# A Perceiver block on one core: the outputs of all units as one pipeline, tile loads across the boundary of the two parts, the first group's rows loaded in the first pass

## The chip, the cores and the metric

One core of one Trainium2 chip runs the whole program. The time is the device time of one execution in microseconds; a kernel is timed in several executions, and their median counts. A profiled execution is one more, with its own time.

## What is computed

128 sequences of 32 tokens with 512 channels pass through three residual layers. All arrays are float32; `ln` is a layer norm without weights.

```python
x = x + xattn(ln(x), ctx_768)   # 16 heads, softmax over 257 context rows of 384 channels
x = x + attn(ln(x))             # gated delta rule, one state of 32x32 per head, a scan over 32 tokens:
#   S = S * a_t;  delta = (v_t - k_t S) * beta_t;  S = S + k_t delta;  y_t = q_t S
#   context = rmsnorm(y) * norm_w * silu(gate);  out = context @ Wo.T + bo
x = x + ffn(ln(x))              # 8 experts of 512x512, the best 2 of each token, softmax of their two logits
```

## The kernel before

The 128 sequences are 32 units of four sequences, 128 token rows each (`NU` = 32); four units are a group (`NG` = 8 groups). The work lies in two passes, each a block in which the five engines (PE, DVE, ACT, POOL and SP, which issues most DMAs) run their own instruction lists and meet by semaphores.

`first_pass` goes over the units: the cross attention of unit u, and beside it the projections of unit u-1. It leaves rows in device memory: `x1` (the first residual sum), `gate`, `qk` and `qsq` for the products, and for the delta rule `kk` and `vb`. DVE solves the delta rule for a group at a time, five units later, as 32 time steps (`time_step`, lines 159 to 173), and SP stores the `deltas` by quarters of the steps. The last turn (unit 32 in `turn`, lines 450 to 487, `last=True`) has only the second half of the last unit and the last quarter of group 6's steps. Group 7's steps are left to the second pass.

`second_pass` (line 1016) has for each unit an **output** job: `y` from `qk` and `deltas` (PE, `make_y`, L1539), its square (ACT, L1328), the mean (DVE, `weighted`, L1400 to L1406), the power -1/2 (POOL, L1301), the scaled context (DVE, L1411), its transposes and the product with `wo` (PE, L1545 and L117), the residual sum with `x1` (DVE, L1419), a layer norm, the expert logits, the choice of two experts (DVE, `choose`), ranks within each expert (PE), the unit's slots (DVE, `place`, L1465), and two indirect DMAs that scatter the rows, scaled by their share, to `slot_rows` by expert (POOL, L1284). A PE `turn` of unit w does pieces of units w+1, w-1 and w-3 in three thirds, so that the engines overlap.

Then come the expert **tiles** of 128 rows: SP loads a tile from `slot_rows` (L1168), PE turns it (`xs_bank`, L1545) and multiplies it by its expert (`mix`, L117), ACT moves it, SP stores it back (L1172). Which expert and which rows a tile has comes from lists that DVE makes (`list_tiles`, L1473 to L1492) when all units of a part are placed; PE and SP read them as register values.

The units are in two parts, 24 and 8 (`UNITS`), with 55 and 23 tiles (`TILES`). Part 0's outputs run alone, turns 0 to 26; turns 24 to 26 only finish units 21 to 23. Then its 55 tiles run, with part 1's turns 24 to 34 among them, 33 thirds from tile 27 on (`inserted`). While the first tiles run, DVE does group 7's time steps; at tile 28 SP stores these deltas, waits for the store and loads group 7. Then SP waits for part 1's lists and scatters, loads the second residual sum of four units, and part 1's 23 tiles run. From the last store of part 0 on, POOL gathers the two expert rows of each unit (L1291, lines 1309 to 1318), DVE adds them to the second residual sum, loaded again (L1180), and SP stores the result (L1189).

```python
def inserted(t):                                            # line 1130
    n = 3 * (UNITS[1] + 3)
    return [(FIRST[1] + i // 3, i % 3) for i in range(n) if INSERT_AT + i * (TILES[0] - INSERT_AT) // n == t]
for part in range(2):                                       # SP, line 1214
    sp.wait_ge(lists_ready, part + 1)
    for i in range(2):
        sp.wait_ge(scattered[i], 16 * (FIRST[part] + UNITS[part]))
for part in range(2):                                       # DVE, line 1501
    first, end = FIRST[part], FIRST[part] + UNITS[part]
    if part == 1:
        for t in range(N):
            time_step(dve, own, tiles, t, t).then_inc(steps_done, 1)
    for w in range(first, end + 4):
```

## Time and profile before

| | us |
|---|---|
| median of 3 runs | 3528.31 (3527.48 to 3530.06) |
| the profiled execution | 3519.57 |
| its span, first to last instruction | 3517.8 |
| PE busy | 3116.7 (89%) |
| DVE busy | 2048.0 (58%) |
| ACT busy | 1131.3 (32%) |
| POOL busy | 987.8 (28%) |
| mean granted TensorE clock | 0.952 of full speed |

The span leaves out 1.8 us around the first and the last instruction of the profiled execution. Busy time of PE is that of its matrix products; weight loads overlap them. Times in the rows below are microseconds from the span's start; "idle before" is the time in which that engine did nothing just ahead of the row, with what ended it. SPq is the issuing of a DMA by SP, not its data. The first pass takes the first 2810 us, and the second pass the rest.

### The profile page before, as it was taken

The numbers are of one execution on the slowest core, as the hardware profiler recorded it, in microseconds if no ns is written. First come the engines' busy times: TensorE is split into PE (matmuls) and PEld (weight loads), VectorE is DVE, ScalarE is ACT, GpSimd is POOL, SyncE is SP. The second block draws the span as 40 slices with busy tenths as digits, with TensorE's granted clock in tenths as the row PEclk, the third lists the DMA queues.
The fourth block names the chain that finished last, engine by engine and source line by source line (L and its number), as shares of the span: only waits on it lengthen the run. The fifth ranks groups of instructions, "written<-read, shape, count | busy, mean of one in ns | idle before, by whom it ended". The sixth has DMA issues, their size and how long they took to land. (4 is left out here: it accounts for less than half of the span.)

```text
span 3517.8 us, 102137 instructions
## 1 busy us (share of the span) xinstructions
PE 3116.7 (89%) x42226; PEld 2288.9 (65%) x42226; DVE 2048.0 (58%) x4203; ACT 1131.3 (32%) x2656; POOL 987.8 (28%) x895
## 2 busy tenths in 40 slices
PE   6999999999999999999999998999899678799975
PEld 5777776767776777777777776777667445444542
DVE  2323366666666666666666666666666658793323
ACT  2333333333333333333333333333333223322321
POOL 2222222222222222222222222222222157502334
PEclk9999999999999999999999999999999878799998
DMA  4222222222222222222222222222221299635469
GB/s 157 83 87 73 89 78 75 75 92 78 75 75 92 78 75 75 92 78 78 72 96 80 75 75 92 78 75 75 92 78 66 70 233 258 211 126 151 138 231 333
DMA packets 297925, 379.11 MB, mean 108 GB/s; under 512 B 159568, under 2 KB 212304, under 8 KB 296016
## 3 DMA queue, kind: packets, MB, share of 16 engines
q1 hardware_dynamic: 287184, 338.19, 30.0%
q0 software_dynamic: 10240, 33.56, 2.8%
q8 instruction: 397, 6.50, 0.8%
q14 instruction: 104, 0.85, 0.1%
HBM read 258.17 MB, written 189.01 MB: 127 GB/s over the span
## 5 line engine op out<-in xcount | busy, mean ns | idle before, releaser
L117 PE MATMUL ring<-cond_high,wkv_high 128*128 128x342 f32 (+1 forms) x1152 | 406.0, 352 | 44.2 <-issue 22.1
L593 ACT ACTIVATE k_t<-ring,kvb 128x342 f32<-128x342 f32 (+1 forms) x384 | 209.5, 546 | 518.2 <-PE ring L117 518.2
L117 PE MATMUL ring<-cond_high,wkv_low 128*128 128x342 f32 (+1 forms) x1152 | 369.0, 320 | 0.0
L117 PE MATMUL ring<-cond_low,wkv_high 128*128 128x342 f32 (+1 forms) x1152 | 368.7, 320 | 0.0
L662 ACT ACTIVATE prob<-score,neg_max 128x257 f32<-128x257 f32 x512 | 236.4, 475 | 314.9 <-DVE neg_max L782 314.9
L117 PE MATMUL ring<-wkv_high,cond_high 128*128 128x512 f32 x768 | 320.5, 417 | 0.0
L170 DVE TENSOR_TENSOR prod<-prod 128x256 f32<-128x256 f32 (+5 forms) x352 | 303.7, 863 | 12.1
L166 DVE TENSOR_TENSOR prod<-coef,deltas 128x64 f32<-128x64 f32 (+30 forms) x248 | 303.0, 1222 | 5.0
L117 PE MATMUL ring<-wkv_high,cond_low 128*128 128x512 f32 x768 | 303.4, 395 | 0.7 <-issue 0.7
L117 PE MATMUL ring<-wkv_low,cond_high 128*128 128x512 f32 x768 | 303.7, 395 | 0.0
L117 PE MATMUL mix<-experts,xs_t 128*128 x624 | 285.9, 602 | 0.0
L117 PEld LDWEIGHTS ring<-cond_high,wkv_high 128*128 128x128 f32 x1152 | 217.8, 189 | 95.9 <-issue 55.0
L895 PE MATMUL turned<-ident,prob 128*128 128x128 f32 x1024 | 152.1, 297 | 108.0 <-DVE prob L789 108.0
L117 PE MATMUL ring<-x1n_t,wattn 128*128 128x128 f32 x2048 | 239.0, 278 | 0.0
L117 PEld LDWEIGHTS ring<-x1n_t,wattn 128*128 128x128 f32 x2048 | 233.8, 194 | 0.0
L117 PE MATMUL ring<-wattn,x1n_t 128*128 128x512 f32 x512 | 230.2, 602 | 0.0
L117 PEld LDWEIGHTS ring<-cond_low,wkv_high 128*128 128x128 f32 x1152 | 218.1, 189 | 15.1 <-issue 15.1
L519 POOL TENSOR_TENSOR tick<-minus_half 128x1 f32<-128x1 f32 x124 | 25.0, 202 | 711.0 <-PE ring L117 711.0
L794 DVE COPY prob_t<-turned 128x512 f32<-128x512 f32 x128 | 88.6, 692 | 228.1 <-PE turned L895 228.1
L112 POOL TENSOR_TENSOR cond_low<-cond,cond_high 128x771 fp32r<-128x771 f32 x128 | 216.5, 1692 | 10.3
L895 PEld LDWEIGHTS turned<-ident,prob 128*128 128x128 f32 x1024 | 131.0, 153 | 134.9 <-DVE prob L789 121.8
L117 PEld LDWEIGHTS ring<-cond_high,wkv_low 128*128 128x128 f32 x1152 | 217.6, 189 | 0.0
(199 smaller groups left out, 5862.4 us busy)
## 6 DMA issues: line engine op xcount, KB each, us to landing
cond<-cond_t_dram SPq DMA_DIRECT2D x128, 385.5 KB, 4.0
xs<-slot_rows SPq DMA_DIRECT2D x78, 256.0 KB, 2.9
slot_rows<-ys SPq DMA_DIRECT2D x78, 256.0 KB, 2.1
x_rows<-x SPq DMA_DIRECT2D x64, 256.0 KB, 3.1
vb_rows<-vgb SPq DMA_DIRECT2D x64, 256.0 KB, 3.2
x_in<-x_dram SPq DMA_DIRECT2D x32, 256.0 KB, 4.7
v_last_s<-v_last_rows SPq DMA_DIRECT2D x512, 0.5 KB
kk_rows<-kk_rows_s SPq DMA_DIRECT2D x32, 256.0 KB, 2.7
```

Source lines behind the costliest of these rows:

```text
L112: return eng.tensor_tensor(low, whole, high.bitcast(F32), ALU.subtract)
L117: last = pe.matmul(out, lhs_t, rhs, start=(i == 0), stop=(i == len(terms) - 1))
L166: own.then(dve.tensor_tensor(tiles["prod"][:, 0:t], coef, tiles["deltas"][:, 0:t], ALU.mult))
L170: own.then(dve.tensor_tensor(tiles["prod"][:, 0:half], tiles["prod"][:, 0:half], tiles["prod"][:, left:whole], ALU.add))
L519: own = Own(pool, pool_steps, lambda: pool.tensor_tensor(tick[:], minus_half[:], minus_half[:], ALU.add))
L593: act.activation(k_t[:, group, at:at + n], ring_bank[bank][:, 0:n], ACT.Identity, bias=kvb[:, group:group + 1]).then_inc(ring.free[bank], 1)
L662: act.activation(prob[:, g, :], score[:, g, 0:M], ACT.Exp, bias=neg_max[:, g:g + 1], accum_out=sums[:, g:g + 1]).then_inc(exp_done, 1)
L794: dve.tensor_copy(prob_t[:, 1, :], turned[1][:]).then_inc(prob_t1_ready, 1)
L895: last = pe.transpose(turned[j][:, g * P:g * P + P], prob[:, g, j * P:j * P + P], ident[:])
```

## The change

It has four parts. One: `qk`, `delta` and `x1` of the second pass move into a tile `shared_rows` that holds the Q weights and the keys in the first pass; SP loads group 0's rows and four units' `x1` into it in the first pass's last turn, after three waits, and no longer at the second pass's start. Two: the turns of the second pass run from 0 to 34 in one line with no end at unit 24; turns 0 to 26 (`BEFORE` = 27) run ahead of the tiles, with everything of units 24 to 27 that falls into them, and turns 27 to 34, 24 thirds, are inserted from tile 32 to tile 49. DVE's group 7 steps come between turns 26 and 27. Three: the tiles run from 0 to 77 in one line; SP's wait for part 1's lists and scatters stands at tile 52, three ahead of the first tile that needs it, the store and load of group 7 at tile 29, the loads of the second residual sum after tile 55's store. Four: POOL sets only the constant -1/2 at first and makes the others after the first unit's bias; PE's waits for weights and constants move to the thirds that use them.

```diff
-INSERT_AT = 27
+BEFORE = NU - GU - 1
+INSERT_AT, INSERT_END = 32, 50
...
+        shared = both.enter_context(nc.sbuf_tensor("shared_rows", [P, DC * D + HG * MU], F32))
+        early = {"qk": shared[:, 0:BU * D].rearrange("p (b n) -> p b n", b=BU),
+                 "delta": shared[:, BU * D:2 * BU * D].rearrange("p (b n) -> p b n", b=BU),
+                 "x1": shared[:, 2 * BU * D:3 * BU * D].rearrange("p (b n) -> p b n", b=4),
...
-        wq = sb("wq", [P, DC, D])
+        wq = shared[:, 0:DC * D].rearrange("p (c n) -> p c n", c=DC)
...
-        k_t = sb("k_t", [P, HG, MU])
+        k_t = shared[:, DC * D:].rearrange("p (g n) -> p g n", g=HG)
...
+                if last:
+                    sp.wait_ge(x1_stored, 16 * NU)
+                    sp.wait_ge(qk_stored, 16 * (NU - 1))
+                    sp.wait_ge(deltas_stored, 16 * ((NG - 1) * GU - 1))
+                    load_group(sp, early, [early["qk"]], [early["delta"]], rows, 0)
+                    for w in range(4):
+                        load_x1(sp, early, rows["x1"], w)
                 if group is None:
                     store_results(u, (u - 1) // GU, (u - 1) % GU)
...
-        qk = sb("qk", [P, 2, BU, D])
-        delta = sb("delta", [P, 2, BU, D])
-        x1 = sb("x1_unit", [P, 4, D])
+        qk = [early["qk"], sb("qk", [P, BU, D])]
+        delta = [early["delta"], sb("delta", [P, BU, D])]
+        x1 = early["x1"]
...
-            n = 3 * (UNITS[1] + 3)
-            return [(FIRST[1] + i // 3, i % 3) for i in range(n) if INSERT_AT + i * (TILES[0] - INSERT_AT) // n == t]
+            n, places = 3 * (NU + 3 - BEFORE), INSERT_END - INSERT_AT
+            return [(BEFORE + i // 3, i % 3) for i in range(n) if INSERT_AT + i * places // n == t]
...
-            load_group(0)
             load_unit(0)
             sp.dma_start(bo_s[:], bo.rearrange("(a n) -> a n", a=1).to_broadcast([P, D])).then_inc(bo_loaded, 16)
-            load_x1(0)
...
-            for w in range(1, 4):
-                load_x1(w)
-            load_group(1)
-            for w in range(UNITS[0] + 2):
-                follow(w, FIRST[0], UNITS[0])
+            load_group(sp, early, qk, delta, rows, 1)
+            for w in range(BEFORE):
+                follow(w)
...
+            tiles_listed(0)
+            at = {t: row_of(t) for t in range(3)}
+            for t in at:
+                load_tile(t, at[t])
+            for t in range(sum(TILES)):
+                if t + 3 == START[1]:
+                    tiles_listed(1)
+                if t + 3 < sum(TILES):
+                    at[t + 3] = row_of(t + 3)
+                    load_tile(t + 3, at[t + 3])
+                if t == INSERT_AT - 3:
+                    sp.wait_ge(steps_done, N)
+                    store_deltas(sp, tiles, rows["deltas"], NG - 1, 0, N).then_inc(deltas_stored, 16)
+                    sp.wait_ge(deltas_stored, 16)
+                    load_group(sp, early, qk, delta, rows, NG - 1)
+                for w, third in inserted(t):
+                    if third == 2 and w < NU + 2:
+                        follow(w)
+                store_tile(t, at.pop(t))
+                if t == START[1]:
                     for i in range(2):
                         sp.wait_ge(x2_stored[i], 16 * NU // 2)
                     for w in range(4):
                         load_x2(w)
...
+            pool.memset(minus_half[:], -0.5).then_inc(half_ready, 1)
+            pool.wait_ge(half_ready, 1)
             pool.wait_ge(bo_loaded, 16)
...
+            for w in range(NU + 4):
...
+                if w == 0:
+                    make_constants()
+                if w + 1 == BEFORE:
+                    scatter(BEFORE - 4)
...
+            for w in range(NU + 4):
+                if w == BEFORE:
+                    place(w - 4)
+                    list_tiles(0)
                     dve.wait_ge(coef_loaded, 16)
                     dve.wait_ge(steps_loaded, 16)
                     for t in range(N):
                         time_step(dve, own, tiles, t, t).then_inc(steps_done, 1)
...
-            pe.wait_ge(outputs_loaded, 32)
-            pe.wait_ge(constants, 1)
-            for w in range(FIRST[0], UNITS[0] + 3):
+            for w in range(BEFORE):
                 for third in range(3):
-                    turn(w, third, FIRST[0], UNITS[0])
+                    if (w, third) == (1, 1):
+                        pe.wait_ge(outputs_loaded, 32)
+                    if (w, third) == (3, 2):
+                        pe.wait_ge(constants, 1)
+                    turn(w, third)
```

How the instructions move shows best in three places. The first is SP at the end of the first pass and the start of the second, where an unconditional branch leads from block to block. Before, the last turn's `x1` store and zero fill are followed by the last results, and group 0 comes after the branches:

```order
L427 DMA x_rows<-x 128x512
L453 DMA slot_rows<-zero_rows 9x4x16384
L435 DMA qsq_rows<-qsq 128x16
L436 DMA kk_rows<-kk_rows_s 128x8x64
L438 DMA qk_rows<-decay 128x512
L441 DMA vb_rows<-vgb 128x8x64 x2
L444 DMA gate_rows<-vgb 128x512
L145 DMA delta_rows<-deltas 128x384
L198 UNCONDITIONAL_BRANCH
L1135 UNCONDITIONAL_BRANCH
L1142 DMA qk<-qk_rows 32x4x512
L1144 DMA delta<-delta_rows 32x8x64 x4
```

Now the group's loads (one quarter of four is shown) and the `x1` loads stand between the zero fill and the results:

```order
L449 DMA x_rows<-x 128x512
L475 DMA slot_rows<-zero_rows 9x4x16384
L212 DMA shared_rows<-qk_rows 32x4x512
L214 DMA shared_rows<-delta_rows 32x8x64 x4
...
L204 DMA shared_rows<-x_rows 128x512 x4
L457 DMA qsq_rows<-qsq 128x16
L458 DMA kk_rows<-kk_rows_s 128x8x64
L460 DMA qk_rows<-decay 128x512
```

The 24 loads moved ahead of six stores of the first pass and of the branch.

The second place is PE at the last turns ahead of the tiles. Before, turns 25 and 26 have only transposes of `x2n`, logits and ranks, and the tiles' first transposes follow:

```order
L1545 MATMUL turn_bank<-ident,x2n 128x128 x4
L117 MATMUL small_bank<-gate,x2n_t 128x8 x4
L117 MATMUL small_bank<-member,earlier 128x8
L117 MATMUL small_bank<-taken,ones 128x8
L1545 MATMUL turn_bank<-ident,x2n 128x128 x4
L117 MATMUL small_bank<-gate,x2n_t 128x8 x4
L117 MATMUL small_bank<-member,earlier 128x8
L117 MATMUL small_bank<-taken,ones 128x8
L1580 MATMUL small_bank<-taken,ones 128x8
L1597 TENSOR_LOAD expert_at
L1597 ISA x2
L1545 MATMUL xs_bank<-ident,xs 128x128 x4
```

Now turn 26 is as full as the ones before it, with `y` of unit 27, the context of unit 25 and its product with `wo`:

```order
L1566 MATMUL turn_bank<-ident,x2n 128x128 x4
L1560 MATMUL y<-shared_rows 32x32 x64
L1566 MATMUL turn_bank<-ident,context 128x128 x4
L118 MATMUL small_bank<-gate,x2n_t 128x8 x4
L118 MATMUL wo_bank<-wo,context_t 128x512 x4
L118 MATMUL small_bank<-member,earlier 128x8
L118 MATMUL small_bank<-taken,ones 128x8
L1601 MATMUL small_bank<-taken,ones 128x8
L1621 TENSOR_LOAD expert_at
L1621 ISA x2
L1566 MATMUL xs_bank<-ident,xs 128x128 x4
```

Four `y` and two `wo` products came in here, ahead of the first tile.

The third place is PE at the last inserted third, that with unit 31's ranks and the totals (L1580 before, L1601 now). Before, part 0's last product stands right ahead of it and the first tile of part 1 right behind, with two tiles' transposes in a row, as at a start:

```order
L117 MATMUL mix<-experts,xs_t 128x512
L117 MATMUL small_bank<-member,earlier 128x8
L117 MATMUL small_bank<-taken,ones 128x8
L1580 MATMUL small_bank<-taken,ones 128x8
L1597 TENSOR_LOAD expert_at
L1597 ISA x2
L1545 MATMUL xs_bank<-ident,xs 128x128 x4
L1597 TENSOR_LOAD expert_at
L1597 ISA x2
L1545 MATMUL xs_bank<-ident,xs 128x128 x4
L117 ISA
L117 MATMUL mix<-experts,xs_t 128x512
```

Now a tile's transposes and products follow as after any third, and the boundary between the parts comes five tiles later:

```order
L118 MATMUL mix<-experts,xs_t 128x512
L118 MATMUL small_bank<-member,earlier 128x8
L118 MATMUL small_bank<-taken,ones 128x8
L1601 MATMUL small_bank<-taken,ones 128x8
L1621 TENSOR_LOAD expert_at
L1621 ISA x2
L1566 MATMUL xs_bank<-ident,xs 128x128 x4
L118 ISA
L118 MATMUL mix<-experts,xs_t 128x512
L118 ISA
L118 MATMUL mix<-experts,xs_t 128x512
```

The ranks moved ahead of tiles 50 to 54, and the start with two transposes in a row is gone.

## Rows read from the trace of the kernel before

**Rows 1.** Windows: us, busy us (and instructions) of each engine, granted clock, DMA share, GB/s.
```profile
2842.00:3043.00 201.00, 180.17 (x3272) 117.06 (x3272) 153.74 (x492) 68.51 (x144) 138.38 (x101) 0.86 0.90 248
...
3186.00:3365.00 179.00, 168.40 (x1580) 92.97 (x1579) 53.09 (x189) 57.60 (x111) 51.65 (x38) 0.98 0.45 144
...
3480.00:3518.00 38.00, 0.30 (x1) 0.00 (x0) 15.22 (x22) 0.60 (x1) 19.02 (x19) 0.55 0.86 295
...
3400.00:3490.00 90.00, 74.07 (x220) 34.21 (x218) 26.67 (x39) 20.79 (x37) 38.85 (x41) 0.97 1.00 353
```

**Rows 2.** Timeline of PE, second pass's start: start us, us, what, [idle before <-releaser].
```profile
2823.76 1.93 PE L1539 MATMUL y<-delta,qk 32*32 32x32 f32 x128 [27.53 <-DMA delta<-delta_rows]
2830.61 3.08 PE L1539 MATMUL y<-delta,qk 32*32 32x32 f32 x218 [4.92 <-DMA gate<-gate_t_dram]
...
2841.72 4.72 PE L117 MATMUL wo_bank<-wo,context_t 128*128 128x512 f32 x6 [0.69 <-ACT context_t L1334]
```

**Rows 3.** Timeline of SP's DMA issues, end of the first pass and start of the second.
```profile
2763.55 0.82 SPq L453 DMA_DIRECT2D slot_rows<-zero_rows  x1
2793.76 0.36 SPq L435 DMA_DIRECT2D qsq_rows<-qsq  x1
...
2810.28 0.35 SPq L1142 DMA_DIRECT2D qk<-qk_rows  x1
...
2820.61 0.45 SPq L1149 DMA_DIRECT2D silu_unit<-gate_rows  x1
...
2826.33 0.50 SPq L1142 DMA_DIRECT2D qk<-qk_rows  x1
...
2841.52 0.45 SPq L1149 DMA_DIRECT2D silu_unit<-gate_rows  x1
```

**Rows 4.** Timeline of DVE: two products with the gate (L1406), two units' slots (L1465).
```profile
2891.64 0.69 DVE L1406 TENSOR_TENSOR context<-y,silu_unit 128x512 f32<-128x512 f32 x1
...
2952.19 0.68 DVE L1406 TENSOR_TENSOR context<-y,silu_unit 128x512 f32<-128x512 f32 x1
...
3042.93 0.17 DVE L1465 CAST slots<-slot 128x2 uint32<-128x2 f32 x1
...
3066.99 0.17 DVE L1465 CAST slots<-slot 128x2 uint32<-128x2 f32 x1
```

**Rows 5.** Timeline of PE around the hold of SP.
```profile
3201.58 1.29 PE L1539 MATMUL y<-delta,qk 32*32 32x32 f32 x128
3202.80 0.65 PE L1545 MATMUL turn_bank<-ident,context 128*128 128x128 f32 x4
...
3207.43 3.60 PE L117 MATMUL wo_bank<-wo,context_t 128*128 128x512 f32 x8
3216.47 1.11 PE L1545 MATMUL xs_bank<-ident,xs 128*128 128x128 f32 x4 [5.45 <-DMA xs<-slot_rows]
```

**Rows 6.** Timelines of DVE after its time steps, and of SP around the hold.
```profile
3188.15 0.69 DVE L1400 TENSOR_REDUCE mean_sq<-y_sq 128x16 f32<-128x512 f32 x1 [6.88 <-ACT y_sq L1328]
...
3193.76 0.33 SPq L1168 DMA_DIRECT2D xs<-slot_rows  x1
...
3213.30 0.34 SPq L1168 DMA_DIRECT2D xs<-slot_rows  x1
```

**Rows 7.** Timeline of PE at the boundary between the parts.
```profile
3380.23 1.11 PE L1545 MATMUL xs_bank<-ident,xs 128*128 128x128 f32 x4 [14.65 <-DMA xs<-slot_rows]
...
3383.00 4.52 PE L117 MATMUL mix<-experts,xs_t 128*128 x8
...
3387.80 3.60 PE L117 MATMUL mix<-experts,xs_t 128*128 x8
...
3391.67 1.88 PE L117 MATMUL mix<-experts,xs_t 128*128 x4
```

**Rows 8.** Timeline of SP at the boundary.
```profile
3370.86 1.76 SPq L1180 DMA_DIRECT2D deltas<-x_rows  x4
```

**Rows 9.** The page's part 5, ACT's moves of the keys: busy us, mean ns | idle before, releaser.
```profile
L593 ACT ACTIVATE k_t<-ring,kvb 128x342 f32<-128x342 f32 (+1 forms) x384 | 209.5, 546 | 518.2 <-PE ring L117 518.2
```

More of the change, by code:

```diff
@@ L1013, in _, with second_pass @@
             turn(NU, last=True)
[L1016 removed]
+def second_pass(nc, ident, early, rows, wo_t, bo, gate_t, expert_t, out):
     with ExitStack() as ctx:
@@ L1149, in load_unit, with follow @@
                     sp.dma_start(dst[:, w % 2], rows[name][unit_rows(w), :]).then_inc(unit_loaded[w % 2], 16)
-            def load_x1(w):
-                sp.dma_start(x1[:, w % 4], rows["x1"][unit_rows(w), :]).then_inc(x1_loaded[w % 4], 16)
-            def follow(w, first, end):
-                if w < end and w + 2 < NU:
+            def follow(w):
+                if w + 2 < NU:
                     sp.wait_ge(y_read, w + 1)
                     load_unit(w + 2)
-                if first <= w - 2:
+                if w >= 2:
                     sp.wait_ge(x2_ready, w - 1)
@@ L1498, in combine @@
                 dve.tensor_tensor(found[:, w % 4, 0], found[:, w % 4, 0], x2_again[:, w % 4], ALU.add).then_inc(out_ready, 1)
-            dve.wait_ge(constants, 1)
-            for part in range(2):
-                first, end = FIRST[part], FIRST[part] + UNITS[part]
-                if part == 1:
+            dve.wait_ge(half_ready, 1)
+            for w in range(NU + 4):
+                if w == BEFORE:
+                    place(w - 4)
+                    list_tiles(0)
                     dve.wait_ge(coef_loaded, 16)
@@ L1508, in _ @@
                         dve.wait_ge(steps_done, t + 1)
-                for w in range(first, end + 4):
-                    if first <= w - 1 < end:
-                        normalised(w - 1)
-                    if first <= w - 2 < end:
-                        residual(w - 2)
-                    if first <= w - 4:
-                        place(w - 4, part)
-                    if w < end:
-                        weighted(w)
-                    if first <= w - 2 < end:
-                        statistics(w - 2)
-                    if first <= w - 3 < end:
-                        choose(w - 3, first)
-                    if first <= w - 2 < end:
-                        scaled(w - 2)
-                list_tiles(part)
+                if 0 <= w - 1 < NU:
+                    normalised(w - 1)
+                if 0 <= w - 2 < NU:
+                    residual(w - 2)
+                if w >= 4 and w != BEFORE:
+                    place(w - 4)
+                if w < NU:
+                    weighted(w)
+                if 0 <= w - 2 < NU:
+                    statistics(w - 2)
+                if w == 3:
+                    dve.wait_ge(constants, 1)
+                if 0 <= w - 3 < NU:
+                    choose(w - 3)
+                if 0 <= w - 2 < NU:
+                    scaled(w - 2)
+            list_tiles(1)
             for w in range(NU):
@@ L1567, in turn @@
                             .then_inc(logits_ready, 1)
-                    if first <= w - 1 < end:
+                    if 0 <= w - 1 < NU:
                         pe.wait_ge(context_moved, w)
@@ L1573, in turn @@
                             .then_inc(wo_ready, 1)
-                if third == 2 and first <= w - 3:
+                if third == 2 and w >= 3:
                     r = w - 3
@@ L1624 @@
+            pe.wait_ge(experts_loaded, 16 * E)
+            expert = expert_of(0)
+            turn_tile(0)
+            for t in range(sum(TILES)):
+                if t + 1 < sum(TILES):
+                    following = expert_of(t + 1)
+                    turn_tile(t + 1)
+                mix_tile(t, expert)
+                expert = following
+                for w, third in inserted(t):
+                    turn(w, third)
 INPUTS = ["x", "cond_t", "cond_last_t", "q_w", "q_b", "kv_w", "kv_b", "proj_w", "proj_b", "attn_w_t", "wa_t",
```

215 lines of the change are left out of this document (92 added, 123 removed).

## The prediction

> **What bounds the kernel now.** I read four views. First the page: PE is busy 89% of the 3517.8 us, and its row of 40 slices is at 8 or 9 tenths through the first pass; the five slices below 8 tenths that are not the first are the first pass's end and parts of the second pass. The change moves work only there, so I cut the second pass into stretches [rows 1]: outputs (2842 to 3043), tiles with inserted outputs (3186 to 3365), the last 23 tiles with DMA engines in full use (within 3400 to 3490) and the tail. In the outputs PE is busy 180 of 201 us at a mean clock of 0.86, with the DMA engines at 0.90: nearly everything is full. In the inserted stretch PE is busy 168 of 179 us: PE sets the time. From 3400 to 3490 the DMA engines are at 1.00 and move 353 GB/s: there bytes set the time as much as PE. Then timelines of PE, SP and DVE around each joint, which follow with the terms.
>
> **Term 1, the start of the second pass.** PE's first output product waits 27.5 us for the first group's rows, and 4.9 us more for the gate weights; the first Wo product starts at 2841.72 [rows 2]. SP shows why [rows 3]: at 2810.28 it starts 20 loads for group 0 (four quarters of one load and four small ones), which take it until 2820.61, then 11 others, then group 1's 20 until 2841.52, and only then the loads of units 2 and 3. The change issues group 0 and four x1 loads in SP's idle time in the first pass: SP has nothing between 2763.55+0.82 and 2793.76. The 24 issues cost 10.3 us (group 0's price) plus 4 at 0.52 us (11 issues from 2820.61 to 2826.33): 12.4 us, up to 17 at the price that group 1's issues had when the queue was full. They end near 2784, ten us before SP's next issue, so I price them at nothing; what covers them is DVE's last time steps, and without that cover 12 to 17 us would return. Their waits are for stores issued no later than 2763.
> What is left ahead of group 1 is 7 issues, 3.6 us, so group 1 starts at 2813.9 and ends 10.3 to 15.2 us later, at 2824 to 2829 instead of 2841.5: 13 to 18 us earlier, and units 2 and 3 with it. On PE's own side, 13.5 us of the first wait lie after 2810.28, and with the 4.9 us 18 would go. The queue is the later of the two: I take **-16 us**, range -9 to -18 (-9 if the DMA engines, at 0.90 through the outputs, let through only what the 3 MB moved out are worth at 353 GB/s, 8.9 us). Moving the constants on POOL behind the first bias delays unit 1 by a few us at a point where PE still waits on unit 0: nothing.
>
> **Term 2, turns 24 to 26.** Today these drain: unit 19's slots are written at 3042.93 and unit 23's at 3066.99, four turns in 24.1 us [rows 4]. With four more output products and two more Wo products they run like full turns. Seven full turns lie between 2891.64 and 2952.19: 8.65 us each. Four take 34.6 us: **+10 us** (0 if the added work fell wholly into the drain's gaps; +14 if PE's whole 13.7 us for it, worked out in term 3, came on top).
>
> **Term 3, less to insert.** The same work leaves the tile stretch: four output products and two units' transposes and Wo products. The rows are 1.29, 0.65 and 3.60 us [rows 5]; 4x1.29 + 2x(0.65+3.60) = 13.7 us, and the wait for ACT before each Wo product, 0.69 us [rows 2], makes it 15. I take **-15 us** (-13 to -17, as other waits go with it or stay). PE is full there, so all of it counts.
>
> **Term 4, the hold of SP.** SP stores the last group's deltas, waits, and issues that group's 20 loads between the load of tile 31 (3193.76) and of tile 32 (3213.30): 19.5 us in which no tile is loaded or stored [rows 6]. PE lives on the three tiles already loaded and on inserted work, and idles 5.45 us [rows 5]. After the change the hold comes one tile later, and the first inserted turn only at tile 32, behind the hold. Nothing fills it but three tiles: the inserted work of that stretch (1.29 + 0.65 + 3.60, and one more 1.29) is no longer cover. **+6.5 us** (0 to +10). The time steps that the hold waits for are done before it in both: DVE idles 6.9 us before 3188.15 [rows 6].
>
> **Term 5, the boundary between the parts.** Between the last tile of part 0 and the first of part 1 PE idles 14.65 us, then two transposes, and the product starts at 3383.00 [rows 7]: 17.4 us from 3365.6. SP starts part 1's loads only once the lists and the last scatter are there (3370.86) [rows 8], which is 5.3 us after PE's last rank product. In the changed kernel that product sits behind tile 49, SP reaches the wait at tile 52, two tiles and a store later, 2x3.87+1 = 8.7 us (the tile pitch is 3391.67-3387.80 [rows 7]). 5.3 is under 8.7: the wait costs nothing, tile 55 is loaded as any other, and **-17 us** follow (-8 if lists and scatter come 9 us later).
>
> **Term 6, the tail.** From the first product of part 1 to the end are 134.8 us now. The first gathers and the first four tile and x2 loads ran in the hole, beside no tile; they now run beside tiles. What comes after part 0's last store is 64 gathers, 32 loads and 32 stores of a unit and 46 tile moves, 174x262,144 bytes = 45.6 MB; at 353 GB/s that is 129 us, and the last 38 us run at 0.86. Near 138 us instead of 134.8: **+3 us** (0 to +10). A rule speaks for more. In the Trainium skill, "DMA: Bandwidth & Descriptors", section "Queues, rings and completion order", each DMA engine takes turns between the queues that have work. By it the eight gathers that start at once would leave SP's queue half the rate, some 176 GB/s by rows 1: tiles 55 to 57 with their x2 loads are 2.6 MB, 15 us instead of 11.6, and the term +6. No row of this trace has that overlap, so the sum goes by the total of bytes.
>
> **Sum.** -16 + 10 - 15 + 6.5 - 17 + 3 = -28.5 us. The profiled execution took 3519.57 us and would take 3491; the median of the runs shown is 3528.31, 8.7 above it, and I carry the difference over: 3499.8, rounded **3500 us**. What a measurement of this kernel can tell from no change is about 0.2%, 7 us.
>
> **Rivals.**
> *The boundary turns into a hold of another kind.* SP's new wait stands ahead of the store of tile 52, so every us that lists and scatters come later than 8.7 us stops stores, then PE; or the gathers that now start at once take the tile loads' bandwidth. For it: the DMA engines at 1.00 from 3400 on. Against: the 5.3 us. If it gives back 12 of the 17 us: 3512 us.
> *The outputs are limited by bytes.* For it: 0.90 DMA share over 201 us. Against: PE also at 90%, and the even 8.65 us turns. Then terms 1 and 2 become -9 and +14: -17.5, 3511 us.
> *The change does less than it says.* One drain, between outputs and the first tile, stays as it is; if the start stays bound by the first unit's chain and the boundary drain only moves to tile 52, terms 1 and 5 shrink to -6 and -5: about -6.5, 3522 us, no change to a measurement.
> *Slower.* The first pass's Q weights and keys move into one tile ahead of all others, so every later tile gets a new address. If that made each of the 31 full turns of the first pass 1.2 us longer, 37 us would come on top: 3537 us. The point from which it decides is 28.5/31 = 0.9 us a turn. For it nothing; against it, the 384 key moves that write there (546 ns in the mean) have 518.2 us of ACT's idle time before them, all of it waiting on PE [rows 9], so a longer move would be hidden.
>
> **How the numbers follow.** Forecast 0.62, boundary 0.15, bytes 0.11, does less 0.06, slower 0.06. The bounds of the terms rarely fall together; half of each way gives about 14 us to the fast side, 3486, and the rivals at 3511 and 3512 need the slow end at 3515. Faster than 0.2%: the first three, 0.88; same 0.06; slower 0.06.
>
> **What would show it.** The first Wo product near 2823 us of the span; unit 23's slots near 3060; first tile product near 3072; one PE idle near 12 us at tile 32; no PE idle over 2 us between tiles 54 and 55; the first product of tile 55 near 3350; the end near 3489. Wrong if the first pass ends later than 2812, if PE's idle at tile 52 to 55 is over 8 us, or if the stretch from tile 55 to the end is over 145 us.

## The result

The changed kernel takes 3500.98 us (median of 4, 3496.33 to 3502.64) and the kernel before 3529.18 (median of 4, 3527.48 to 3534.02): the ratio given with the result is 0.9904, 95% interval 0.9889 to 0.9918, and the two medians alone divide to 0.9920. Forecast were 3500 us and 3486 to 3515. In a second set, on one chip, it was 3496.08 (6 runs) against 3530.99 (11 runs): ratio 0.9907, interval 0.9888 to 0.9926. So the change gains 28 to 35 us, 0.8 to 1.0%.

### The profile after

The profiled execution of the changed kernel took 3502.01 us (span 3500.2), only 17.6 less than that of before. That gap between profiles and medians is the first thing to explain; the stage table below does it. First the lines that answer to those shown of before.

Windows of the changed kernel: outputs, tiles with inserted turns, the last 23 tiles, the tail (columns as in [rows 1]):

```profile
2832.00:3035.00 203.00, 182.31 (x3335) 118.55 (x3337) 152.50 (x492) 68.41 (x144) 137.69 (x101) 0.85 0.85 246
3188.00:3360.00 172.00, 157.68 (x1053) 86.81 (x1052) 44.67 (x180) 54.49 (x107) 38.34 (x33) 0.96 0.46 150
3390.00:3460.00 70.00, 64.85 (x195) 30.05 (x194) 21.80 (x32) 19.00 (x33) 30.50 (x33) 1.00 1.00 358
3462.00:3500.00 38.00, 0.59 (x2) 0.00 (x0) 15.22 (x22) 0.60 (x1) 18.97 (x19) 0.54 0.88 301
```

The stages are the same and as full as before [rows 1]: TensorE (PE) at 90% of the outputs, DMA engines at 1.00 beside the last tiles. What changed is at the joints.

TensorE at the start of the second pass (answers to [rows 2]):

```profile
2813.30 1.45 PE L1560 MATMUL y<-shared_rows 32*32 32x32 f32 x90 [12.73 <-PEq L220]
2816.66 1.88 PE L1560 MATMUL y<-shared_rows 32*32 32x32 f32 x128 [1.90 <-issue]
2823.69 1.88 PE L1560 MATMUL y<-shared_rows 32*32 32x32 f32 x128 [5.16 <-issue]
2829.08 0.75 PE L1560 MATMUL y<-shared_rows 32*32 32x32 f32 x38 [3.51 <-issue]
...
2831.66 6.38 PE L118 MATMUL wo_bank<-wo,context_t 128*128 128x512 f32 x8 [0.78 <-ACT context_t L1356]
```

The first output product starts the moment the second pass does and waits for no rows. But three pauses without any wait ("issue"), 10.6 us in sum, stand before the first Wo product. Before, there was one such pause in the same place, in a row that [rows 2] leave out:

```profile
2839.24 0.75 PE L1539 MATMUL y<-delta,qk 32*32 32x32 f32 x38 [5.55 <-issue]
```

So 5 of the 10.6 us are new.

SP over the same time, the moved loads in the first pass included (answers to [rows 3]):

```profile
2766.47 0.82 SPq L475 DMA_DIRECT2D slot_rows<-zero_rows  x1
2768.13 0.34 SPq L212 DMA_DIRECT2D shared_rows<-qk_rows  x1
...
2770.45 5.88 SPq L212 DMA_DIRECT2D shared_rows<-qk_rows  x1
...
2785.50 1.89 SPq L204 DMA_DIRECT2D shared_rows<-x_rows  x4
2796.70 0.34 SPq L457 DMA_DIRECT2D qsq_rows<-qsq  x1
...
2813.27 0.34 SPq L1171 DMA_DIRECT2D silu_unit<-gate_rows  x1
...
2832.02 0.45 SPq L1171 DMA_DIRECT2D silu_unit<-gate_rows  x1
```

The 24 moved issues take 2768.13 to 2787.4, 19 us where up to 17 were priced (one alone 5.88), and end 9 us before SP's next issue at 2796.70: the cover held. The store of zeros just ahead of them already stands 2.9 us later than before, so the second pass starts 3.0 us later (2813.27) for a reason ahead of the change.

TensorE and SP at the hold (answer to [rows 5] and [rows 6]):

```profile
3204.00 3.60 PE L118 MATMUL mix<-experts,xs_t 128*128 x8
3217.52 1.11 PE L1566 MATMUL xs_bank<-ident,xs 128*128 128x128 f32 x4 [9.92 <-DMA xs<-slot_rows]
3218.43 5.79 PE L118 MATMUL mix<-experts,xs_t 128*128 x8
```

```profile
3197.75 0.33 SPq L1187 DMA_DIRECT2D xs<-slot_rows  x1
3198.13 0.43 SPq L146 DMA_DIRECT2D delta_rows<-deltas  x1
3203.19 0.34 SPq L212 DMA_DIRECT2D qk<-qk_rows  x1
...
3214.40 0.37 SPq L1187 DMA_DIRECT2D xs<-slot_rows  x1
```

SP loads no tile for 16.65 us (19.5 before), with nothing inserted to cover it, and TensorE idles 9.92 us in place of 5.45. The product behind this idle takes 5.79 us where others take 3.60; the granted clock from 3217.5 to 3222 is 0.50, the lower of its two levels (1.2 and 2.4 GHz).

TensorE at the boundary of the parts and behind it (answers to [rows 7]; the products are those of tiles 54, 55 and 58, the transposes those of tiles 56 and 59):

```profile
3356.36 3.60 PE L118 MATMUL mix<-experts,xs_t 128*128 x8
3359.80 0.60 PE L1566 MATMUL xs_bank<-ident,xs 128*128 128x128 f32 x4
3360.24 3.60 PE L118 MATMUL mix<-experts,xs_t 128*128 x8
...
3376.49 1.11 PE L1566 MATMUL xs_bank<-ident,xs 128*128 128x128 f32 x4 [4.92 <-DMA xs<-slot_rows]
3377.40 4.81 PE L118 MATMUL mix<-experts,xs_t 128*128 x8
```

Tile 54 (3356.36) and tile 55 (3360.24) follow each other at the tiles' pitch. Three tiles later TensorE idles 4.92 us on a late tile load, and the product behind it takes 4.81 us; no profile of before has an idle over 1.6 us behind its first tiles there.

### The stages, over several profiles

S is SP's first DMA issue of the second pass. Each stage is the difference of two times of the timelines: S, the slots of units 19 and 23 (DVE), ACT's moves of the products of tiles 26 and 54, the end. In us:

| profile | S | S to first Wo | S to unit 19 | 19 to 23 | 23 to tile 26 | tile 26 to 54 | 54 to end | S to end |
|---|---|---|---|---|---|---|---|---|
| before | 2810.3 | 31.4 | 232.6 | 24.1 | 119.2 | 178.8 | 152.8 | 707.5 |
| before, second | 2807.2 | 31.7 | 240.4 | 24.8 | 119.2 | 186.1 | 154.5 | 725.0 |
| before, third | 2818.0 | 31.4 | 238.7 | 24.3 | 118.8 | 186.5 | 155.5 | 723.9 |
| changed | 2813.3 | 18.4 | 221.7 | 34.3 | 119.0 | 171.7 | 140.2 | 687.0 |
| changed, second | 2809.5 | 20.0 | 218.2 | 32.2 | 119.6 | 171.0 | 142.0 | 683.0 |

The first profile of before is 17 us quicker behind S than the two others. Read against all three, the second pass gained 34 us, not 20.

### The profile page after: what moved, and what is told of

Same layout as the page of the kernel before. It is cut to its first block and busy times, and to the rows that moved or that the text cites. A ratio compares the mean times of both kernels' runs of the same rounds, so it can differ in the third digit from the quotient of the medians.

```text
span 3500.2 us, 102140 instructions
## 1 busy us (share of the span) xinstructions
PE 3121.0 (89%) x42226; PEld 2290.5 (65%) x42226; DVE 2048.1 (59%) x4203; ACT 1130.3 (32%) x2656; POOL 987.8 (28%) x895
## 5 line engine op out<-in xcount | busy, mean ns | idle before, releaser
L622 ACT ACTIVATE shared_rows<-ring,kvb 128x342 f32<-128x342 f32 (+1 forms) x384 | 209.3, 545 | 516.9 <-PE ring L118 516.7
L171 DVE TENSOR_TENSOR prod<-prod 128x256 f32<-128x256 f32 (+5 forms) x352 | 301.5, 857 | 12.1
L548 POOL TENSOR_TENSOR tick<-minus_half 128x1 f32<-128x1 f32 x124 | 24.8, 200 | 709.3 <-PE ring L118 709.3
```

The costliest lines, as they stand in the source:

```text
L171: own.then(dve.tensor_tensor(tiles["prod"][:, 0:half], tiles["prod"][:, 0:half], tiles["prod"][:, left:whole], ALU.add))
L548: own = Own(pool, pool_steps, lambda: pool.tensor_tensor(tick[:], minus_half[:], minus_half[:], ALU.add))
L622: act.activation(k_t[:, group, at:at + n], ring_bank[bank][:, 0:n], ACT.Identity, bias=kvb[:, group:group + 1]).then_inc(ring.free[bank], 1)
```

## The experiments

**before_again and before_third.** The kernel before, unchanged, profiled twice more.

> The kernel before, profiled a second time. The two profiles shown are 17.6 us apart (3519.6 and 3502.0), the medians 28.2 us. If the profiled execution of before shown was a short one by chance, this one lies nearer its median, at 3525 to 3532, and the extra 5 to 12 us lie in stages that the change doesn't touch. If profiled executions of before are always short, it is 3520 again. The store of the last x1 rows in the first pass, issued at 2763.1 in before and 2766.1 in the changed kernel, tells whether the first pass differs between the kernels: at 2763 again the shared addresses lengthen the first pass by 3 us, at 2766 or more it is chance.

> The kernel before, profiled a third time, for the spread of its stages. From the two profiles at hand: second pass's first issue to unit 19's slots 232.6 and 240.4 us, moves of tile 26 to tile 54 (the stretch with the inserted turns) 178.8 and 186.1, move of tile 54 to the end 152.8 and 154.5. If the stretch with the inserted turns is what scatters, by windows in which TensorE's granted clock falls below 1.00, it comes out between 176 and 188 here, longer the more such windows it has, and the tail stays at 152 to 155; if the scatter is spread over all stages alike, the tail moves too.

Spans 3532.2 and 3541.8, executions of 3534.0 and 3543.6 us: longer than the 3525 to 3532 that I expected, and longer in stages that the change does touch. The first profile was a short one, and the places where it was short are the outputs (232.6 against 240.4 and 238.7) and the stretch with the inserted turns (178.8 against 186.1 and 186.5). The tail moves by 3 us only. The windows of 100 us behind tile 31, first of the profile of before, then of the second and the third:

```profile
3222.00:3272.00 50.00, 48.74 (x544) 27.14 (x543) 13.06 (x49) 16.36 (x32) 11.37 (x8) 1.00 0.45 144
3272.00:3322.00 50.00, 48.35 (x424) 26.96 (x423) 18.40 (x70) 17.52 (x35) 20.21 (x15) 1.00 0.40 133
```

```profile
3228.00:3278.00 50.00, 47.10 (x529) 25.82 (x528) 10.79 (x42) 15.31 (x30) 11.36 (x8) 0.97 0.41 138
3278.00:3328.00 50.00, 47.15 (x413) 26.06 (x412) 17.41 (x63) 15.76 (x31) 20.20 (x15) 0.97 0.37 122
```

```profile
3236.00:3286.00 50.00, 47.05 (x529) 25.82 (x528) 10.51 (x41) 14.97 (x30) 11.36 (x8) 0.97 0.43 137
3286.00:3336.00 50.00, 46.65 (x413) 26.19 (x412) 17.70 (x65) 16.20 (x31) 20.10 (x15) 0.97 0.37 122
```

The quick profile has the clock at 1.00 throughout and TensorE at 97%; the others have a mean of 0.97 and TensorE at 94%. Behind the hold an idle came ahead of the lower clock; whether an idle or the clock came first in these windows, no run tells. As for the first pass: the store of the last x1 rows is issued at 2760.0 and 2770.8 in these two profiles, and S lies at 2807 to 2818 in the three profiles of before and at 2807 to 2821 in the eleven of the changed kernel and its variants, so the 3 us of the first pair are within the scatter, and the shared addresses cost nothing that shows.

**after_again, start_undone, boundary_undone**, on one chip.

> The changed kernel again, as the base of the next two runs: 0.990 of before. By chance in the first pass its store of the last x1 rows moves by a few us; if the shared addresses are the cause, it stays at 2766. No PE idle over 2 us at tiles 52 to 55, about 5 us of idle at tile 58, and about 10 at tile 32.

Measured: 3496.08 us, S at 2809.5, no idle at tiles 52 to 55, 4.75 us at tile 58, 9.54 at tile 32: all as in the first profile of this kernel, and the first pass's 3 us gone.

start_undone takes the moved loads out of the last turn and puts them back at the second pass's start:

```
-                if last:
...
-                    load_group(sp, early, [early["qk"]], [early["delta"]], rows, 0)
-                    for w in range(4):
-                        load_x1(sp, early, rows["x1"], w)
...
+            load_group(sp, early, qk, delta, rows, 0)
             load_unit(0)
...
+            load_x1(sp, early, rows["x1"], 0)
...
+            for w in range(1, 4):
+                load_x1(sp, early, rows["x1"], w)
             load_group(sp, early, qk, delta, rows, 1)
```

> The changed kernel with group 0's rows and the first four x1 rows loaded at the second pass's start again. By the prediction's term the time rises by 16 us over the changed kernel. By the lower end of that term (the transfers of the start are limited by bytes) it rises by 9. By the profile of the changed kernel, where the first product of the second pass comes 13 us earlier behind its start, it rises by 13 and the first product stands 28 us behind the pass's first issue, as before. By the rival of the shared addresses (slower first pass), which stay in this kernel, nothing of the first pass changes.

Measured: 3508.17 us (6 runs, 3500.54 to 3509.92), 12.1 over the changed kernel. Its stage from S to unit 19 is 233.0, 13 over the mean of the two profiles of the changed kernel (220.0); the others stay. So the early rows are worth 12 to 13 us: between the two bounds of the term. TensorE's rows in it:

```profile
2819.93 3.08 PE L1557 MATMUL y<-shared_rows 32*32 32x32 f32 x218 [27.04 <-DMA shared_rows<-delta_rows]
2827.27 1.88 PE L1557 MATMUL y<-shared_rows 32*32 32x32 f32 x128 [4.26 <-issue]
2833.48 0.75 PE L1557 MATMUL y<-shared_rows 32*32 32x32 f32 x38 [4.34 <-issue]
```

The first 218 products come in one piece here, and the first pause is missing; in the changed kernel the first piece is 90 products, then 1.9 us of pause. What TensorE took in while it waited for rows, it now has to wait for by itself.

boundary_undone drains SP, TensorE and ScalarE between tiles 54 and 55 (SP's part of the edit):

```
-                if t + 3 < sum(TILES):
+                if t + 3 < START[1] or START[1] <= t < sum(TILES) - 3:
                     at[t + 3] = row_of(t + 3)
                     load_tile(t + 3, at[t + 3])
...
                 store_tile(t, at.pop(t))
-                if t == START[1]:
+                if t + 1 == START[1]:
+                    tiles_listed(1)
...
+                    for i in range(START[1], START[1] + 3):
+                        at[i] = row_of(i)
+                        load_tile(i, at[i])
```

> The changed kernel with a drain between tiles 54 and 55 as before: x2 loads and the tile loads of the second part follow the store of tile 54, and TensorE and ScalarE take up tile 55 behind tile 54's product. By the prediction's terms for the boundary (17) and the tail (gives back 3) the time rises by 14; by the rival that the boundary's gain goes to gathers and bytes behind it, it rises by 5 at most, since the tail from the first product of tile 55 to the end shrinks from 140 us to 125 or so. PE idles 10 to 15 us ahead of tile 55 in both; the tail's length tells.

Measured: 3504.72 us (6 runs), 8.6 over the changed kernel; the stage from tile 54 to the end is 149.8, 8.7 over the mean of the two (141.1). TensorE ahead of tile 55:

```profile
3349.35 7.03 PE L118 MATMUL mix<-experts,xs_t 128*128 x16
3364.55 1.11 PE L1570 MATMUL xs_bank<-ident,xs 128*128 128x128 f32 x4 [8.17 <-DMA xs<-slot_rows]
```

8.17 us of idle where before had 14.65 [rows 7]: since the inserted turns end at tile 49, lists and scatters are long there, and this drain is shorter than the old one. So of the 13 us that the last stage lost (154.3, the mean of the three of before, to 141.1), 8.7 are the missing drain, and some 4 are left for the earlier end of the turns, which no run tried by itself. Neither theory had that split: one gave 14, the other 5 at most.

**group1_late, hold_spread, x2_early, stores_later**, in a later set. These four take up the pauses, the hold and the idle at tile 58.

```
             load_unit(1)
-            load_group(sp, early, qk, delta, rows, 1)
             for w in range(BEFORE):
                 follow(w)
+                if w == 1:
+                    load_group(sp, early, qk, delta, rows, 1)
```

> The changed kernel with group 1's twenty loads issued behind unit 3's (they are first needed by turn 3) and not ahead of unit 2's. Theory A, transfers hold up the start: TensorE's gaps between the pieces of the first three y (1.9 to 2.7, 4.9 to 5.2 and 3.0 to 4.6 us in three profiles of kernels with the early rows, with no wait to explain them) shrink with 1.3 MB less under way, the first Wo product comes 3 to 6 us sooner behind the second pass's first issue (18 to 20 us in those profiles), and the whole gains as much. Theory B, TensorE's own intake of instructions sets the gaps: they stay at 10 us in sum, the first Wo product stays at 18 to 20 us, and the time is the changed kernel's within 0.1%, since unit 2's rows, though 12 us sooner, wait behind the first residual on VectorE. Theory C: group 1 comes too late for turn 3, and y of unit 4 waits: 3 to 8 us slower.

Measured: 3495.06 us (6 runs): the changed kernel's time. TensorE's rows:

```profile
2812.24 1.46 PE L1561 MATMUL y<-shared_rows 32*32 32x32 f32 x90 [12.30 <-PEq L220]
2815.59 1.88 PE L1561 MATMUL y<-shared_rows 32*32 32x32 f32 x128 [1.90 <-issue]
2822.90 1.88 PE L1561 MATMUL y<-shared_rows 32*32 32x32 f32 x128 [5.43 <-issue]
2826.37 0.75 PE L1561 MATMUL y<-shared_rows 32*32 32x32 f32 x38 [1.59 <-issue]
```

Unit 2's rows are issued at 2818.61, 6.4 us behind S and not 18.8, and the first Wo product still comes 16.7 us behind S. So SP's queue is not what holds the start: Theory B in the main. Of Theory A one trace is left: the last pause, beside which no transfer of group 1 runs now, is 1.59 us, against 2.4 to 4.6 in the nine other profiles with early rows, while the middle one, beside Wo's megabyte, stays at 5.43. Theory C fell.

```
-                if t == INSERT_AT - 3:
+                if t == INSERT_AT - 6:
                     sp.wait_ge(steps_done, N)
                     store_deltas(sp, tiles, rows["deltas"], NG - 1, 0, N).then_inc(deltas_stored, 16)
+                if INSERT_AT - 4 <= t < INSERT_AT:
                     sp.wait_ge(deltas_stored, 16)
-                    load_group(sp, early, qk, delta, rows, NG - 1)
+                    load_group(sp, early, qk, delta, rows, NG - 1, [t - INSERT_AT + 4])
```

(Here `load_group` takes the quarters that it is to load as one more argument.)

> The changed kernel with the last deltas stored at tile 26 and group 7 loaded five rows at a time at tiles 28 to 31, and not both at tile 29. If SP's hold of 17 us costs the idle of 9.5 to 10 us on TensorE at tile 32, as my term for the hold has it, that idle goes to under 2 us, and the time falls by 8 to 11 us with the product at a low clock behind it. If the y of group 7 would have waited there anyway (deltas stored late), the idle moves to the first y of turn 27 and less than 3 us is gained.

Measured: 3490.11 us (5 runs), 5.0 under group1_late beside it and 6.0 under the changed kernel's 3496.08; in the trace the idle is gone and the stage from tile 26 to 54 is 160.6, 10.8 under the 171.4 of the changed kernel (mean of two):

```profile
3207.16 3.60 PE L118 MATMUL mix<-experts,xs_t 128*128 x8
3210.60 0.60 PE L1567 MATMUL turn_bank<-ident,x2n 128*128 128x128 f32 x4
3211.61 1.29 PE L1561 MATMUL y<-delta,qk 32*32 32x32 f32 x128 [0.41 <-DMA delta<-delta_rows]
```

The first y of group 7 waits 0.41 us: the hold, not the deltas, had been the cost. The trace shows all that was expected; the medians show 5 to 6 us of the 8 to 11, and scatter over 7 to 13 us.

x2_early changes one number (`if t == START[1] - 4:` for the four x2 loads), stores_later another (`- 5` in place of `- 2` in `combined`).

> The changed kernel with the first four x2 rows loaded at tile 51 and not at 55. If the idle of 4.8 us at tile 58 comes from transfers that share the engines (x2's 1 MB, eight gathers of 256 KB and the tiles' rows at once), 1 MB less leaves 2 us of idle, and the tail from the move of tile 54 to the end (140 to 142 us in two profiles) shrinks by 2 to 3 us, which are 1 MB at 360 GB/s. If SP's wait for the first combined unit causes it (the store of unit 0's output stands in SP's queue ahead of tile 60's load), the idle stays, and the tail too.

> The changed kernel with each store of a combined unit three tiles later in SP's order. If SP's wait for the first combined unit causes the idle at tile 58, the idle goes, but the gathers behind the stores start 12 us later, so the tail from the move of tile 54 to the end is longer or as long: what limits it is bytes (0.96 to 1.02 of the transfer engines from 3390 on). If TensorE's tiles set the end of the tail, the idle goes and the tail shrinks by 5 us. If transfers cause the idle, it stays at 3 to 5 us.

Measured: x2_early 3493.56 us (6 runs), the idle at tile 58 gone, tail 135.2 us: 5.9 less, twice what 1 MB is worth at 360 GB/s. The idle of 4.92 us and the 1.2 us that the product behind it took too long (4.81 for 3.60) make that up. In the medians it is 2.5 us under the changed kernel and 1.5 under group1_late, which 6 runs each don't tell from nothing. TensorE at the place:

```profile
3367.84 3.60 PE L118 MATMUL mix<-experts,xs_t 128*128 x8
3371.31 0.63 PE L1566 MATMUL xs_bank<-ident,xs 128*128 128x128 f32 x4
3371.77 3.60 PE L118 MATMUL mix<-experts,xs_t 128*128 x8
```

stores_later 3503.32 us (6 runs): the idle stays (4.69), and the tail is 152.2, 11 longer. So the four x2 loads cause the idle, not SP's wait for the first combined unit. Whether it is by their bytes alone no run tells: in the changed kernel their issues also take SP 1.87 us (from 3364.94) just ahead of tile 59's load (3367.55). And whoever stores later gathers later.

**hold_and_x2, x2_kept and eight_places.** The two edits that helped, together; then with x2 of 16 units kept in buffers that are read out; then with eight places for gathered units and x2 of 8 units kept. Of the last two edits the main lines:

```
+        keep = [early["qk"], early["delta"], qk[1], delta[1]]
...
+            def keep_x2(w):
+                sp.wait_ge(y_ready, 28 if w < 12 else 32)
+                sp.wait_ge(x2_stored[w % 2], 16 * (w // 2 + 1))
+                sp.dma_start(x2_at(w), rows["x2"][unit_rows(w), :]).then_inc(x2_kept[(w - 4) // 8], 16)
```

```
+        keep = [qk[1], delta[1]]
+        places = [found[:, i] for i in range(4)] + [early[n][:, 2 * i:2 * i + 2] for n in ("qk", "delta") for i in range(2)]
```

> The changed kernel with both edits that helped: group 7's rows spread over tiles 28 to 31 (stretch of the inserted turns 171 to 160.6 us), and the first x2 rows at tile 51 (tail from the move of tile 54 to the end 141 to 135 us). If the two costs are apart from each other, both gains add: 10.5 + 6 = 16 us below the changed kernel, 3481. If the tail is limited by the bytes it must move alone, whenever TensorE gets there, the tail is 135 again; if it was limited by when part 1's tiles come, it grows.

> The former, with x2 of units 4 to 19 loaded into the buffers of groups 6 and 7 when these are read out (tiles 4 to 11 and 42 to 49), where the transfer engines are at half share or less, so that 4 MB fewer move in the tail. If bytes limit the tail, it loses 4 MB at 360 GB/s, 11 us: from 135 to 124, and the whole comes to 3470. If the round trips of the four gather buffers limit it (gather, sum, store, each waiting for the one before), it stays over 131. If TensorE's 23 tiles at 3.87 us and the last units behind them limit it, it ends at 125 to 130.

> The kernel with both edits (group 7's rows spread, the first x2 rows at tile 51; 3487.0 us, tail from the move of tile 54 to the end 135.6 us), with eight places for gathered units in place of four (four of them in the buffers of group 6, read out before the tiles) and x2 of units 4 to 11 kept in those of group 7. The tail took 135.4 us with 4 MB fewer to move, so bytes alone don't set it. If the round trips of the four places do (gather, two sums, store, each behind the one before), the tail falls to 118 to 128, and the whole to 3470 to 3480. If the tiles' own loads and stores and the orders of SP set it, it stays at 133 to 137. If sixteen gathers at once hold up the tiles' loads, TensorE idles by over 5 us behind tile 58, and the tail is 135 to 145.

Measured: hold_and_x2 3487.02 us (4 runs; ratio to before 0.9863, interval 0.9841 to 0.9885), stages 164.0 and 135.6: the gains add in the trace but for 3 us, while the median is 9 us under the changed kernel, and 16 were expected. x2_kept 3484.44 (4 runs) and eight_places 3483.96 (4 runs) were expected at 3470, and at 3470 to 3480: they gain 3 us more, which 4 runs each don't tell from nothing. Their tails are 135.4 and 134.9. The first rules out bytes as the only limit and left the round trips (over 131). The second rules out the round trips as the only limit; it fits the tiles' own loads and stores and SP's orders (133 to 137), and its TensorE still idles, 4.33 us behind tile 59 and 2.57 two tiles on. Windows from the move of tile 55 or so to the last tile, and from there to the end, of hold_and_x2, x2_kept and eight_places:

```profile
3360.00:3454.00 94.00, 86.75 (x261) 40.45 (x259) 29.07 (x42) 24.73 (x43) 43.28 (x46) 1.00 0.98 345
3454.00:3491.00 37.00, 0.58 (x2) 0.00 (x0) 15.23 (x22) 0.60 (x1) 19.55 (x18) 0.56 0.89 303
```

```profile
3354.00:3447.00 93.00, 87.28 (x260) 41.47 (x258) 29.07 (x42) 24.10 (x43) 43.72 (x46) 0.98 0.91 305
3447.00:3485.00 38.00, 0.37 (x1) 0.00 (x0) 15.22 (x22) 0.60 (x1) 18.33 (x19) 0.54 0.87 293
```

```profile
3347.00:3446.00 99.00, 89.56 (x261) 42.05 (x259) 31.94 (x47) 24.48 (x43) 48.58 (x48) 0.97 0.93 320
3446.00:3478.00 32.00, 0.25 (x1) 0.00 (x0) 11.73 (x17) 0.60 (x1) 15.53 (x16) 0.58 0.88 310
```

With fewer bytes the share falls (0.98 to 0.91) but not the time: bytes are not what is left of the tail. With eight places the part behind the last tile is 5 us shorter and the tiles ahead of it 4 to 6 longer, while sixteen gathers start beside them. What is left of the 135 us is then the 23 tiles at 3.87 us (89), transfers in their way (8 to 14), and a chain of 32 to 38 behind the last tile, where the last eight units are gathered and those and the ones ahead of them summed and stored. That chain took 37 to 38 us in the kernel before too, so nothing that the change gained in the last stage came from there. It was not tried apart, and stays open.

## Why the prediction was right, and which steps were not

The total came out within a microsecond of the first median and 4 over the second. By its own steps, with the forecast, the first pair of profiles, and the means of the profiles in the table (3 of before, 2 of the changed kernel):

| terms | forecast | first pair | means |
|---|---|---|---|
| 1, to unit 19 | -16 | -10.9 | -17.3 |
| 2, unit 19 to 23 | +10 | +10.2 | +8.8 |
| 3 and 4, tile 26 to 54 | -8.5 | -7.1 | -12.4 |
| 5 and 6, tile 54 to end | -14 | -12.6 | -13.2 |

**The frame.** The sum was made against a profile 8.7 us under the median, and the 8.7 were carried over. That worked by luck in part. For the profile the sum gave 3491 us, and 3502.01 was measured: it promised 28.5 us, and the first pair shows 17.6. The median came out because the changed kernel's profile lies 1.0 us over its median and not 8.7 under. The three profiles of before differ by 24 us. A sum that is made against one execution has its scatter in every term that is a stretch and not a gap. So the signs in the profile came late: the first Wo product at 2831.66 for 2823, unit 23's slots at 3069 for 3060, the first product of tile 55 at 3360.24 for 3350, the end at 3500.2 for 3489, with 3.0 us of each from the first pass.

**Term 1** is right in its sign and mis-sized: with the loads put back the kernel is 12.1 us slower, not 16. The step that failed is "The queue is the later of the two". SP's queue did come free 9.5 us sooner in the profile (2841.52 to 2832.02), and 12.5 sooner behind S, close to the 13 to 18 forecast; but making it free 12 us sooner still (group1_late) changed the median by 1.0 us, within the scatter. TensorE's side is the later: the forecast had it lose 18 us, 13.5 for rows and 4.9 for the gate weights. The rows' part came true. The wait for the gate weights went too, but the pauses grew by as much, from one of 5.55 us to three of 10.6 us in sum, and the forecast had no room for the new ones: from the first y to the first Wo product it is 18.4 us now and was 18.0. So it lost 13.0 in the first pair (31.4 to 18.4 behind S). The other end, 9 us by bytes, is too low by 3. The 17.3 us in the means hold some of the outputs' scatter. The moved waits and constants were not undone by themselves; start_undone keeps them, and its first Wo product comes 29.5 us behind S for 31.4, so they are worth some 2 us there.

The pauses come after 90, 218 and 346 products in every profile with early rows (in start_undone after 218 and 346, before after 346 alone), and each product brings a weight load: 128 products are 256 instructions. The transfers of the changed kernel's instruction queue from 2813 to 2830:

```profile
q8 instruction: 3, 0.05, 1.3%
```

Three packets, 0.05 MB, for three pauses. They begin between 2814 and 2815, 2820 and 2821, 2826 and 2827. In all ten profiles one such packet ends within each pause, 1.1 to 2.0 us ahead of the next product; before, two of the three fell into the waits for rows and for gate weights, and only the last into a pause. The Trainium skill, "Runtime: NRT & Kernel Launch", section "Instruction fetch mechanics", says that a sequencer takes its program in blocks of 16 KiB, 256 instructions each, through a DMA queue of its own, and that this is mostly hidden. Spacing and packets agree with the first part; here it is not hidden: the three pauses are 8.9 to 12.5 us in sum. That they are this intake is read from the spacing and the times of the packets, and not shown by a run that takes them away.

**Term 2** stands: four turns in 34.3 us, 8.6 each, where 34.6 were forecast.

**Terms 3 and 4.** By the first pair -7.1 for -8.5. The hold cost 4.5 us more idle (9.92 for 5.45), priced at 6.5. That leaves 11.6 us for term 3 by the first pair and 16.7 by the means, where 15 were forecast; no run undid the moved outputs, so terms 2 and 3 rest on stages alone. Against the two slower profiles of before the stage gained 15: there the granted clock had a mean of 0.97 behind tile 31. The seven profiles whose hold is the changed kernel's take 171.0 to 171.7, the three of before 178.8 to 186.5: with the denser turns the stretch also scatters less. Whether the density is the cause wasn't tried.

**Term 5** stands: no idle at tiles 52 to 55, SP's wait for lists cost nothing, and the first product of tile 55 came 3.9 us behind that of tile 54. What it is worth is split otherwise than I had it (boundary_undone: 8.7 for the drain; the rest is left for turns that end sooner).

**Term 6** was priced at +3 by bytes and measured +5.2 (tile 55's first product to the end, 134.8 to 140.0). The idle of 4.92 us at tile 58, beside eight gathers and the x2 loads, is what was added, and 1 MB less at that place took 5.9 us off the tail in the trace, not the 2.9 that its bytes are worth. The rule of the Trainium skill that I weighed there, "DMA: Bandwidth & Descriptors", section "Queues, rings and completion order", that engines take turns between queues, gave +6: place and size agree with it better than with my sum of bytes, and from 3368 to 3376 the gathers' queue took 46.6% of the engines and SP's 54.3%, near the half that the rule gives. But the x2 loads' 1.87 us of issues and 2.9 us of bytes, both ahead of tile 59's load, make 4.8 us too, so the size does not decide between the two.

**The rivals.** The boundary that becomes another hold came true in small, as the idle at tile 58, 5 us and not 12. Against outputs limited by bytes speak start_undone, which costs 12 and not 9, and the turns at 8.6 us. "Does less than it says" and "slower" fell: the first pass's length is the same over 14 profiles within its scatter. My sign for being wrong, a first pass that ends later than 2812, came up (2813.3) and was a bad one: before itself starts its second pass at 2807 to 2818.

## What to carry to other kernels

Profile the kernel before more than once ahead of a sum: in three profiles of before the drain was 14.65, 15.04 and 14.92 us and the hold's idle 5.45, 5.27 and 5.56, while the outputs and the stretch with the inserted turns each scattered by 8 us. Only the gaps could be priced from one trace. When loads are moved ahead of a block, look at what the engine itself did while it waited for them; it may need part of that time anyway. Joining two stages puts the transfers of both side by side: move those that can go early (four x2 loads, a group in pieces of five loads) into a stretch where the engines are at half share.

## What was not expected of the hardware

- TensorE pauses at the start of the second pass for 1.6 to 6.3 us behind each 256 instructions (128 weight loads and products), in all ten profiles with early rows, and once, for 5.2 to 5.6 us, in each profile of before; later y of the same 256 instructions run through in 1.29 us.
- One DMA issue on SP took 5.5 to 6.0 us in the last turn, the sixth behind the store of zeros, in all ten profiles with early rows, where most take 0.35 to 0.5.
- Two edits, one that moved 4 MB out of the tail and one that moved 2 MB out and doubled its buffers, left it at 135 us within 0.7, at a transfer share of 0.87 to 0.93.
